# Unread fp32 products on TensorE ahead of and among the transposes of every normalisation

## The reference, cut to what matters

```
def _layernorm(x, axis=-1, eps=1e-05):
    m = jnp.mean(x, axis=axis, keepdims=True)
    v = jnp.var(x, axis=axis, keepdims=True)
    return (x - m) / jnp.sqrt(v + eps)

x = x + _L0_attn_ref(_layernorm(x, axis=-1), ...)
x = x + _L0_xattn_ref(_layernorm(x, axis=-1), ctx_1024, ...)
x = x + _L0_ffn_ref(_layernorm(x, axis=-1), ...)
...
x = x + _L3_ffn_ref(_layernorm(x, axis=-1), ...)
```

## Time and profile before

| what | value |
|---|---|
| runs of the kernel before | 1481.42, 1482.19, 1483.22 us |
| the profiled execution's own time | 1480.64 us |
| its span, first to last instruction | 1478.9 us |
| PE busy | 1089.0 us (74%), 6339 products |
| DVE (VectorE) busy | 897.1 us (61%) |
| ACT (ScalarE) busy | 575.7 us (39%) |
| POOL (GpSimd) busy | 449.6 us (30%) |
| mean granted TensorE clock | 0.834 of full speed |

### The profile page before, as it was taken

The page is one execution under the profiler, slowest core; times in us unless marked ns, Lnnn a source line. Parts: engine busy times, 40 slices in busy tenths (PEclk is TensorE's granted clock), DMA queues, the critical chain, the costliest instruction groups (busy, mean ns, idle before and its releaser), DMA issues. The chain is left out here.

```text
span 1478.9 us, 18967 instructions
## 1 busy us (share of the span) xinstructions
PE 1089.0 (74%) x6339; PEld 655.6 (44%) x6339; DVE 897.1 (61%) x2266; ACT 575.7 (39%) x1616; POOL 449.6 (30%) x411
## 2 busy tenths in 40 slices
PE   5883999996730006883668699867589999999975
PEld 4352988983510003461236545447133444444423
DVE  5556677764709945547544420254888888898602
ACT  1242677772110002231232133211534666666662
POOL 4014355541006622211100000000556555565200
PEclk9696899997955556795579889959787999999996
DMA  6500000000070010000000300000000000000000
GB/s 161 140 1 1 1 2 1 1 2 1 1 89 0 0 23 0 2 2 0 1 1 0 110 5 1 1 1 1 0 0 1 1 1 1 1 2 1 1 0 12
DMA packets 54318, 20.97 MB, mean 14 GB/s; under 512 B 27001, under 2 KB 52941, under 8 KB 54221
## 3 DMA queue, kind: packets, MB, share of 16 engines
q1 hardware_dynamic: 54220, 19.76, 6.2%
HBM read 17.29 MB, written 2.46 MB: 13 GB/s over the span
## 5 line engine op out<-in xcount | busy, mean ns | idle before, releaser
L492 DVE TENSOR_REDUCE L3x_MH<-L3x_pM 100x1 f32<-100x482 f32 (+1 forms) x384 | 235.4, 653 | 35.7 <-PE L3x_pM L707 33.8
L601 ACT ACTIVATE L3x_E<-L3x_pS 128x400 f32<-128x400 f32 (+1 forms) x384 | 174.3, 501 | 92.9 <-PE L3x_pS L728 89.7
L707 PE MATMUL L3x_pM<-ctx_tm 128*100 128x482 bf16 (+1 forms) x384 | 150.9, 403 | 4.8 <-DVE L3x_MH L492 4.3
L728 PE MATMUL L3x_pS<-ctx_tm 128*128 128x400 bf16 (+1 forms) x384 | 126.8, 337 | 8.8 <-ACT L3x_E L601 5.8
L354 POOL TENSOR_SCALAR L3x_T<-L3x_X,cols 128x482 bf16<-128x482 f32 (+2 forms) x58 | 83.3, 1437 | 143.9 <-DVE L3x_X L479 84.4
L1571 ACT ACTIVATE L0x_E<-L0x_E,ctx_r 128x100 f32<-128x100 f32 x288 | 105.0, 368 | 6.3 <-DVE L0x_E L1493 6.3
L2072 PE MATMUL L1a_pT<-ident,L1a_OX 100*128 100x100 f32 x8 | 1.8, 384 | 134.7 <-DMA L1a_OX<-regroup_out 134.7
L707 PEld LDWEIGHTS L3x_pM<-ctx_tm 128*100 128x100 bf16 x384 | 49.0, 128 | 104.5 <-DVE L3x_MH L492 78.2
L759 PE MATMUL L3x_pO<-L3x_E,L3x_V 128*32 128x400 f32 (+1 forms) x768 | 85.0, 515 | 0.0
L1417 POOL TENSOR_TENSOR L0x_E<-L0x_E,L0x_RZ 128x1200 f32<-128x1200 f32 x24 | 52.6, 2192 | 74.3 <-DVE L0x_RZ L1513 74.3
L1645 PE MATMUL L0x_pS<-L0x_QS,CT 128*128 128x100 f32 x576 | 73.3, 287 | 0.0
(11 more groups left out here) (610 smaller groups left out, 2494.7 us busy)
## 6 DMA issues: line engine op xcount, KB each, us to landing
ctx_tm<-in_ctx SPq DMA_DIRECT2D x8, 704.0 KB
ctx_tm<-in_L_ffn_wi SPq DMA_DIRECT2D x4, 512.0 KB, 7.7
ctx_tm<-in_L_ffn_wo SPq DMA_DIRECT2D x4, 512.0 KB, 7.8
regroup_in<-CT SPq DMA_DIRECT2D x8, 200.0 KB
L1a_L<-regroup_in SPq DMA_DIRECT2D x4, 400.0 KB, 8.1
w_f0g<-in_L_ffn_Wg SPq DMA_DIRECT2D x1, 512.0 KB
w_f0u<-in_L_ffn_Wu SPq DMA_DIRECT2D x1, 512.0 KB
w_f0d<-in_L_ffn_Wd SPq DMA_DIRECT2D x1, 512.0 KB
```

What stands on the lines that cost most here:

```text
L492: nc.vector.tensor_reduce(MH[:, b % 2, j, g, c:c + 1], pM[0:T, n % 3, 0:CH[c]], AX.X, ALU.max, negate=True).then_inc(s_mr, 1)
L601: nc.scalar.activation(E[0:tiles[k], n % EB, :], pS[0:tiles[k], n % 2, 0:NG * T], ACT.Exp, scale=SCALE8).then_inc(s_e, 1)
L707: last = nc.tensor.matmul(pM[0:T, n % 3, 0:CH[c]], QS[:, j, g, b * T:(b + 1) * T], KS[:, b % KB, j // 2, k0:k0 + CH[c]], start=True, stop= ...
L728: last = nc.tensor.matmul(pS[0:tiles[k], n % 2, 0:NG * T], KS[:, b % KB, j // 2, k * 128:k * 128 + tiles[k]], QS[:, j, :, b * T:(b + 1) * ...
```

## The change

`ln_tensor` issues 26 more fp32 products in each of the eleven stages that call it: 20 ahead of the first transpose, and one behind each transpose except the fourth and the eighth. Each multiplies `m.ident` (stationary, 128 columns) by 112 columns of `m.ones` and writes columns 400 to 511 of a bank of the transposes, which nothing reads. They wait for nothing and signal nothing. Nothing else is changed.

```
 def ln_tensor(nc, pe, m, q, banks, src=None):
 
     src = m.XN if src is None else src
+    keep_warm(nc, m, banks[1], 20)
     for b in range(B):
         pe.wait_ge(q.norm, b + 1)
         nc.tensor.transpose(banks[b // HB][:, (b % HB) * T:(b % HB + 1) * T], src[:, b, :],
                             m.ident[0:T, 0:T]).then_inc(q.xT, 1)
+        if b % HB < HB - 1:
+            keep_warm(nc, m, banks[b // HB], 1)
+
+
+def keep_warm(nc, m, bank, n):
+
+    for _ in range(n):
+        nc.tensor.matmul(bank[:, HALF:512], m.ident[:, :], m.ones[:, 0:512 - HALF], start=True, stop=True,
+                         skip_group_check=True)
```

## The result

The changed kernel takes 1486.05 us (median of nine runs, 1483.15 to 1489.7), the kernel before 1482.19 (nine runs beside it, 1480.98 to 1483.22). The ratio is 1.0025, with an interval of 1.0013 to 1.0037: slower by about 0.25%. The forecast was 1478.5 us, so its sign was wrong. The time lies in its range (1473.5 to 1489).

What follows compares the result with a forecast made beforehand. No engine fills the span: time is a sum of barrier-closed stages, with TensorE often at 1.2 GHz. Gains led by L0f and L3f, less losses led by L1x, sum to -3.7 us, so 1478.5 us; range 1473.5 to 1489.

Steps and rivals of the forecast that it cites:

- the cover: Idle time ahead of the transposes, under VectorE's statistics and GpSimd's power: the twenty were to cost 0 in seven stages.
- L1x, +1.9 forecast: Stage L1x: the twenty, not covered, take 2.4 us; first reader directly behind the copy: +1.9 us, bounds +1.4 and +3.8.
- L3x, +1.0 forecast: Stage L3x: the twenty covered, clock low again at the transposes, the six delay the reader of XNT: +1.0 us.
- No slack: Stage L3x: the reader of XNT starts 0.70 us behind the transposes, about what the copy takes, so delay passes on.
- L3f, -3.0 forecast: Stage L3f: clock rises near the first transpose and shortens the chain of products: -3.0 us, bounds +1.96 and -3.7.
- L0f, -4.0 forecast: Stage L0f: clock rises near the first transpose, ScalarE's first two activations come earlier: -4.0 us, bounds +0.97 and -4.4.
- L0a, -0.5 forecast: Stage L0a: late by 0.5 us, then two or three products halved by the clock: -0.5 us, bounds +1.5 and -1.5.
- L2f and L3a, +0.97 each forecast: Stages L2f and L3a: TensorE idle behind the twenty, clock low, the eighth transpose late: +0.97 us each.
- L2a, -0.8 forecast: Stage L2a: clock still high at the first eight products gives 0.8 us: -0.8, bounds 0 and -5.
- L1a and L1f 0, L2x -0.2: L1a limited by its queue's transfers, L1f's delay covered: 0 each; L2x: low clock costs 0.5, a rise gives 1.3: -0.2.
- too late: Rival, every stage: clock not risen at the first transpose, pairs slower than VectorE's pace; +10.7, so 1493, or 1489; chance 0.17.
- The -8.5 of my side calculation: Sum if the skill's load rule held: the twenty take 2.1 us at either clock, 4.8 us of delays vanish; -8.5, not -3.7.

Runs made afterwards that it cites:

- the second profile: The changed kernel run once more with no edit, for a second profile: 1485.17 us against 1481.84 for the kernel before, ratio 1.002; profiled run 1485.92 us.

## Why the prediction was wrong

**The step that failed is the price of an added product.** I read the earlier trace rows as 17 and 20 products. They are records. The line of the earlier trace rows has 576 of them, and the code issues 24 x 12 = 288 products there: I had the row that says so and didn't count it against the loop. One fp32 product is two records at 0.213 us each at the low clock, 0.112 at the high one. The distances were right, and the number was off by two. Twenty cost 8.5 us at 1.2 GHz and 4.5 at 2.4, not 4.26 and 2.24; measured are 4.69 to 7.60 in the changed kernel, whose clock rises on the way. A transpose is one record (x8 for eight), so a pair with a product costs three, not two: 0.62 us at the low clock where I had 0.426, and 0.32 where I had 0.224. With it went the cover: a run priced at 4.26 us seemed to fit the idle time of seven stages.

What this did to each term:

- *L1x, +1.9 forecast, +5.39 and +6.05 measured.* The run lasts 5.42 us, not 2.4. The twenty are what costs here: by the profiles they give +3.24 alone, the six alone -0.14. Counted from the start of the stage, the first reader comes at 10.0 us before and 14.1 after, 4.1 late. The clock rises (at 8.2 and 8.4 us) where it did before, so the run buys nothing. The remaining 1.3 us, in both profiles, lie behind the first reader. The clock falls at 22.1 us and rises again at 56.2, against 18.5 and 49.2 before, so the low stretch is 3.4 us longer; that this is their cause wasn't tested. This term also lay outside the bounds I had given it (+1.4 and +3.8).
- *L3x, +1.0 forecast, +4.25 and +3.78 measured.* "No slack" was right and the low clock was right. The eighth transpose starts 3.90 us behind the first instead of 2.77; before it was 1.51 here (1.94 - 0.43, by the earlier trace rows), not the 1.80 that I used. The six are what costs: by the profiles they give +3.38 alone, the twenty alone +0.27. How much follows isn't fixed: with ten ahead and the six the reader is just as late, but the clock rises at 16.2 us, and the stage takes 0.90 more. The first reader is 2.2 us later in its stage, and the clock's rise 3.6 us (at 22.4 us instead of 18.8). The kernel without the addition in L3x and L1x confirms the two together: 1.002 becomes 0.9974, or some 6.8 us.
- *L3f, -3.0 forecast, -0.14 and -1.54 measured.* The gain was sized well. From the first reader of XNT to the end the stage is 3.2 us shorter; I had 3.1. But that reader comes 3.1 us later in its stage, where I had taken 0.1.
- *L0f, -4.0 forecast, -2.29 and +0.50.* In the first profile the step is exact: from L1860 to the second activation took 360.73 - 352.32 = 8.41 us and takes 359.13 - 354.72 = 4.41, which is the 4.0. The first product is 1.7 us later in its stage, and that is the difference. In the second profile the clock falls back and takes the gain too.
- *L0a, -0.5 forecast, +1.55 and +2.44.* Late by 2.37 and 2.95 us instead of 0.5.
- *L2f and L3a, +0.97 each forecast; -1.7 and -1.4 measured.* The same mistake with the other sign. I let the twenty end long before the transposes, with TensorE idle between and the clock low. They are 7.60 and 6.86 us long, reach the transposes (0.70 and 0.06 late), and the clock is 1.00 through them and the products behind. That alone doesn't make the gain. The clock falls again in both stages, and the length goes with its last rise. In L3a that rise comes at 38.6 us into the stage here, at 39.8 before, and at 43.3 in the kernel undone in L1x and L3x (+2.15 us). In L2f it comes at 23.0 here, 26.0 before, and 28.5 with ten and the six (+2.23).
- *L2a, -0.8 forecast, -3.0 measured*, within the bounds. But 2.2 to 3.7 us are gained here in every kernel tried, also in those with the six alone and with bf16, so the run ahead can't be the main reason. What they have in common is the last rise: 20.1 to 21.3 us into the stage in all eleven profiles, 29.7 in the one of the kernel before, where TensorE works without a gap at 1.2 GHz for nine microseconds more. Before, and then the changed kernel:

```profile
730.40:739.60 9.20, 9.20 (x42) 3.07 (x42) 5.28 (x11) 5.05 (x12) 0.00 (x0) 0.50 0.00 1
734.70:743.80 9.10, 8.90 (x56) 3.41 (x48) 7.32 (x15) 7.04 (x17) 0.00 (x0) 1.00 0.00 1
```

  With one profile of the kernel before, that late rise may be its own chance, and part of this gain with it.
- *L1a and L1f 0, L2x -0.2*: -0.1, -0.6 and +0.2 in the first profile, near the forecast; the slack behind the transposes covered 1.5 and 2.1 us of lateness. For L1a and L2x that is partly luck: over the other kernels they lie between -3.2 and -0.4 and between -2.1 and +3.2.

The five first terms miss by 13.4 us in the first profile. L2a, L2f and L3a give back 7.2, all other stages together nothing. That is the way from -3.7 to +2.5; from the profile that lies nearer the median it is +5.3.

**What was right.** The clock does rise within the run, and it is full at the transposes in ten of eleven stages (the exception is L3x). So the rival "too late", whose 1489 lies nearest to the time, isn't what happened in the changed kernel: there the transposes were late because the added run was long, not because the clock was low. It is what happened to the kernel with the six alone. Its mechanism, pairs slower than VectorE's pace, was priced at +10.7, and that kernel is 11.2 us slower; the agreement is partly chance, since each pair costs more than I had said and slack hides some of it.

**What is left of the mechanism with the run that I had in mind.** Ten fp32 products are 20 records and last about 4.2 us, as forecast for twenty. With the six the ratio is 0.9983, without them 0.9978: 1479.98 and 1477.66 us, on either side of my 1478.5. By the profile with the six L0f and L3f come out near their terms (-3.49 for -4.0, -3.19 for -3.0) and L3x too (+0.90 for +1.0), while L1x, L2f and L3a lose 10.5 us where I had 3.8, and L1a, L2a and L2x give 6.2 where I had 1.0. So the agreement of the time is partly luck. How far the clock holds behind a run of that length isn't sure either: in L0f it holds with the six and falls without them. With twenty short records (bf16) neither L0f nor L3f gains (+0.10 and -0.11), and the ratio is 0.9994. The six, for which I had allowed 2.9 us in L2f, L3a and L3x, cost 10.6 beside the twenty. The -8.5 of my side calculation was wrong in itself: it let all delays vanish, though a run of 2.1 us would still stand on the path in L1x.

**Still open.** The changed kernel's own runs spread over 6.5 us, and whether the clock falls back in L0f moved 2.8 us between two profiles; what decides that wasn't found. The clock also moves stretches in which nothing was added: the short one ahead of L1f takes 11.4 us where the clock is full throughout (the kernel before, the twenty without L1x and L3x), and 12.5 to 13.5 in the ten other profiles, which are at 0.50 for 2.0 to 4.0 us in it. How much of the loss in L1x behind its first reader is clock and how much is waiting wasn't separated.

## What to carry to other kernels

Before a duration per product is taken from a group of the trace, divide its record count by what the loop issues; for fp32 products it is two here. Unread work that raises the clock pays where it fills idle time and runs on into the real work. Over the whole kernel a little too long was better than a gap (0.9932 against 0.9961), though not in every stage (L0a). Transposes that are all ready catch up 1.2 us of a late start, and nothing should stand between them: the six cost 10.6 us. Put no run where TensorE already works up to the point (L1x, +3.24 us for the twenty alone), and expect nothing of one behind which it is idle for long (L3x, +0.27). The additions in those two stages alone turned a gain into a loss.

## What the runs showed of the hardware

- An fp32 product of 128 stationary columns is two loads and two products, a bf16 one a single pair (52 records against 26 for the same loop). The products of 400 columns take 1.33 us for two records at 1.2 GHz, which is 4 x 400 columns at that clock. The Trainium skill, "FP8 and Floating Point Precision", section "TensorE Precision Notes", counts "4 passes through PE array" for true FP32. The trace agrees, with two passes to a record. By it the twenty would be 20 x 4 x 128 columns at 1.2 GHz, an estimate of 8.5 us (with the 128 columns of the load, which fit the 0.213 us of a record; 112 would give 0.187). The records give the same, 40 x 0.213.
- The bf16 products are 0.093 us apart at 1.2 GHz, which is their 112 moving columns at that clock; the fp32 records are 0.213 apart, which is twice 128 columns.
- An fp32 transpose stays one record, at 0.25 us when the clock is full and 0.37 to 0.43 when it is not; eight that are ready start within 0.60 us.
- A clock that has risen can fall back under dense work: in L0f of the second profile PE was busy for 6.32 of 6.90 us at 0.99, and then for all of 3.40 us at 0.51.
